# Attention over graph segments: the segment maxima are turned between columns and rows by VectorE, and the sets of zeros between gathers go

## The chip, the cores and the metric

The kernel runs on one core of a Trainium2 chip. A core has a matrix engine (TensorE, PE in the profile), a vector engine (VectorE, DVE), a scalar engine (ScalarE, ACT), a general engine that also issues the indirect gathers (GpSimd, POOL), and SyncE (SP), which issues plain transfers here. Each engine works through its own queue in order, and they wait for each other by semaphores. The metric is the device time of one execution in microseconds, the median of three runs.

## The reference

Four graph layers follow each other over 3125 nodes with 256 features and 100,000 edges sorted by destination. Layers 0 (two rounds) and 3 are graph attention with four heads. What is computed in one round of layer 0:

```python
e = jax.nn.leaky_relu(alpha_s[src] + alpha_d[dst], NEG_SLOPE)
m = jax.ops.segment_max(e, dst, num_segments=N)
ex = jnp.exp(e - m[dst])
s = jax.ops.segment_sum(ex, dst, num_segments=N)
alpha = ex / (s[dst] + 1e-16)
out = jax.ops.segment_sum(h[src] * alpha[:, :, None], dst, num_segments=N)
```

Layer 3 is the same with segments by source and each logit times the edge's weight. Layer 1 takes the logits from dot products of the two ends, and layer 2 sums messages without a softmax. Those two have code of their own.

## The kernel before

The work runs in stages behind each other. Three of them are calls of the function `attend`: tags `0a` and `0b` for the two rounds of layer 0 (kind "self", `own_max`: each node is also its own neighbour), and stage 3, whose names have no tag in the profile, for layer 3 (kind "weighted"). Edges are laid out in 816 units of 128, so that no unit crosses a group of 128 nodes. A turn handles STEP = 16 units in four quads of four, and there are 51 turns, three to a loop body.

A turn in `attend` goes like this. GpSimd gathers 128 table rows of 260 numbers for each unit into `ring` (L1520), which holds three turns. Behind each gather it sets a buffer named `pause` to zero (L1524, 128x256), which nobody reads; it waits by `paused` for its own sets of zeros and by `rows` for VectorE to free the ring. SyncE loads indices, masks and totals of units (`masks`, `totf`, `totb`, `tot_last`). TensorE turns the gathered scores so that 64 partitions (4 heads by 16 units) hold 128 edges each (`scores`), and VectorE adds the two parts (`y`, L1597), `leaky`, `withself` or `weigh`.

Then the maximum of each segment has to reach all its edges, also where a segment runs over several units. VectorE does this by scans. `fwd` scans each unit from its first edge; the last value of each unit goes to one line over the units, where `carried` scans it on and gives each unit the maximum it begins with (`begin`); `full` scans with that; `bwd` scans back; its first values go to a line again, `back` scans that, and gives `end`; `top` is then each edge's segment maximum. Between a column over 64 partitions and a line on one partition the numbers make a trip through TensorE: `trip1` to `trip4` (L1709), each a transpose into PSUM, and VectorE reads it back with a copy (`col1`, `begin`, `col2`, `end`, all at line L111 of a helper). `under`, `firsts` and `shrink` then make the differences, ScalarE takes `exp`, TensorE turns the result (`back_turned`) together with the factor by which the maximum has moved on, and ScalarE copies it out (`alphas`).

The same turn also sums the units of the turn before, while the maxima of this one are made. VectorE multiplies the gathered rows of a quad by their weights (`rows0` to `rows3`, L1577), ScalarE builds one-hot matrices of the edges' nodes in two steps (`away`, `hot`) and adds the weights' own columns (`ext`), TensorE multiplies the two (`mm0` to `mm15`, L1700, four PSUM banks in turn), and VectorE adds each result to its group of nodes (`add0` to `add15`, L1571). `factor` (L1672) and `rescale` (L1587) start the next turn's sums. The numbers of the groups come from a table and are loaded to registers in VectorE's queue (L1557) before `y`. TensorE also spreads the nodes' scores to edges (`spread0`, `spread1`), joins them (`joined`), and runs filler matmuls whose result nobody reads (`keep_busy`: 6 behind `scores`, 8 behind `trip2`, 8 behind `spread1`).

The order on each engine is written by hand: lists `V`, `A` and `M` name the steps of a turn on VectorE, ScalarE and TensorE. On VectorE the pieces of the maxima stand between the adds: `fwd`, `rows1`, `add0` to `add3`, `col1` to `carry`, `add4` to `add7`, `rows2`, `begin` to `bwd`, `rows3`, `add8` to `add11`, `col2`, `back`, `end` to `shrink`, `add12` to `add15`, `factor`. On ScalarE `exp` stands behind `hot3`, `ext3` (which wait for `mm7`) and `hot_r1`; `alphas`, `away0`, `hot0`, `parts`, `picked`, `own` follow.

## Time and profile before

| | us |
|---|---|
| median of three runs | 8620.68 |
| lowest and highest of them | 8600.65, 8642.47 |
| the profiled execution's own time | 8664.63 |
| its span, first to last instruction | 8662.7 |

| engine | busy, us | share of the span |
|---|---|---|
| TensorE, matmuls | 5621.8 | 65% |
| VectorE | 4989.0 | 58% |
| ScalarE | 3877.8 | 45% |
| GpSimd | 5844.0 | 67% |

Busy time is a sum over all stages, and no engine comes near the whole span, so what sets the time has to be read stage by stage, from the waits. A matmul's end is modelled in the profile; a time at which another engine goes on that waited for it is measured. Waiting and register instructions aren't counted as busy. Queues of plain transfers (SP) and of GpSimd's gathers share the 16 DMA engines; the gathers' queue took 27.5% of them and the other large one 9.3%.

### The profile page before, as it was taken

Reading aid. Unit: us, or ns where it says so; the run is one execution under the profiler, and the core shown is the slowest. Engines: PE = TensorE matmul, PEld = TensorE weight load, DVE = VectorE, ACT = ScalarE, POOL = GpSimd, SP = SyncE. Lnnn points to the kernel's source line nnn. Section 1 sums busy time; section 2 is a strip of 40 time slices with the busy share of each in tenths; the row PEclk is TensorE's granted clock in tenths of the full one; section 3 lists DMA queues with packets and bytes.
Section 4 is the critical chain, followed back from the end, with each engine's and each line's share of the span. In section 5 each row is a group of like instructions: output and inputs, shape, how many; then the busy total and the mean of one; then the engine's idle time right before and its main releaser. Section 6 shows DMA issues by size and latency. Waiting matters only on the chain. (4 is left out here: it accounts for less than half of the span.)

```text
span 8662.7 us, 136659 instructions
## 1 busy us (share of the span) xinstructions
PE 5621.8 (65%) x25128; PEld 3980.1 (46%) x25129; DVE 4989.0 (58%) x11551; ACT 3877.8 (45%) x9075; POOL 5844.0 (67%) x8186
## 2 busy tenths in 40 slices
PE   6442367667646666773677777748787763667765
PEld 5441244444424444442555555535555542444444
DVE  6445255556545555553777887754444444566666
ACT  2230255555424555552344444425555542555554
POOL 0556677777747777775466776757777765888884
PEclk9999687887767888776889998968888875788887
DMA  4111333333313333330466666523333322334442
GB/s 145 50 51 41 83 101 101 100 100 101 86 45 102 101 101 101 101 101 21 139 172 173 185 176 173 145 62 100 102 101 101 102 74 81 106 105 109 107 108 76
DMA packets 582372, 894.76 MB, mean 103 GB/s; under 512 B 308788, under 2 KB 359137, under 8 KB 581877
## 3 DMA queue, kind: packets, MB, share of 16 engines
q0 software_dynamic: 245984, 649.30, 27.5%
q1 hardware_dynamic: 335876, 218.84, 9.3%
q10 hardware_dynamic: 416, 25.60, 0.9%
q8 instruction: 30, 0.49, 0.0%
q14 instruction: 66, 0.53, 0.0%
HBM read 859.36 MB, written 59.47 MB: 106 GB/s over the span
## 5 line engine op out<-in xcount | busy, mean ns | idle before, releaser
L2024 POOL DMA_INDIRECT ad_ring<-tab_qv,ad_idx x808 | 768.8, 951 | 496.8 <-issue 242.1
L2440 POOL DMA_INDIRECT ae_ring<-tab_a,ae_idx x808 | 777.9, 963 | 399.4 <-PE ae_po L2597 199.9
L1520 POOL DMA_INDIRECT at_ring_0a<-tab_s,at_idx_0a x808 | 771.1, 954 | 368.6 <-DVE at_rows_0a L1577 207.3
L1520 POOL DMA_INDIRECT at_ring_0b<-tab_s,at_idx_0b x808 | 772.4, 956 | 349.8 <-DVE at_rows_0b L1577 174.1
L1520 POOL DMA_INDIRECT at_ring<-tab_s,at_idx x808 | 781.3, 967 | 272.8 <-issue 119.0
L2590 PE MATMUL ae_pM<-ae_we,ae_featT 64*128 64x256 f32 x1616 | 501.8, 461 | 211.2 <-issue 169.2
L1700 PE MATMUL at_po_0a<-at_rows_0a,at_hot_0a 128*128 128x264 f32 x1616 | 559.5, 504 | 101.1 <-DVE at_begin_0a L111 28.4
L1700 PE MATMUL at_po_0b<-at_rows_0b,at_hot_0b 128*128 128x264 f32 x1616 | 551.5, 499 | 110.7 <-DVE at_begin_0b L111 32.7
L1700 PE MATMUL at_po<-at_rows,at_hot 128*128 128x260 f32 x1616 | 540.9, 492 | 111.8 <-DVE at_begin L111 27.0
L2218 PE MATMUL ad_pk<-node_a,ad_hr 128*128 x1616 | 459.9, 433 | 210.7 <-DVE ad_prod L2101 107.7
L565 POOL DMA_INDIRECT recs_s<-rnk_recs_now,rnk_pos_now x294 | 288.3, 981 | 400.7 <-DVE rnk_both L465 178.2
L2590 PEld LDWEIGHTS ae_pM<-ae_we,ae_featT 64*128 64x128 f32 x1616 | 347.3, 226 | 348.3 <-issue 214.2
L2550 DVE TENSOR_TENSOR ae_pre<-ae_ring,ae_pM 128x1024 f32<-128x1024 f32 x202 | 246.7, 1221 | 445.4 <-PE ae_pM L2590 260.1
L2256 PE MATMUL ad_po<-ad_ring,ad_hot 128*128 128x264 f32 x1616 | 480.2, 429 | 32.4 <-ACT ad_hot L2329 11.5
L2597 PE MATMUL ae_po<-ae_msg,ae_hot 128*128 128x256 f32 x1616 | 453.2, 431 | 52.9 <-issue 37.6
L1700 PEld LDWEIGHTS at_po_0a<-at_rows_0a,at_hot_0a 128*128 128x128 f32 x1616 | 382.0, 249 | 218.3 <-issue 74.9
L1700 PEld LDWEIGHTS at_po_0b<-at_rows_0b,at_hot_0b 128*128 128x128 f32 x1616 | 375.9, 245 | 225.4 <-issue 72.4
L2397 DVE TENSOR_TENSOR acc<-acc,ae_po 128x256 f32 x808 | 290.8, 417 | 323.5 <-PE ae_po L2597 167.3
L1700 PEld LDWEIGHTS at_po<-at_rows,at_hot 128*128 128x128 f32 x1616 | 372.8, 243 | 216.3 <-issue 63.7
L2218 PEld LDWEIGHTS ad_pk<-node_a,ad_hr 128*128 128x128 f32 x1616 | 329.5, 213 | 306.2 <-issue 259.9
L1571 DVE TENSOR_TENSOR acc<-acc,at_po_0a 128x264 f32 x808 | 312.8, 421 | 231.7 <-PE at_pb_0a L1719 85.5
L1571 DVE TENSOR_TENSOR acc<-acc,at_po_0b 128x264 f32 x808 | 312.2, 421 | 209.8 <-PE at_pb_0b L1719 65.2
(538 smaller groups left out, 14649.4 us busy)
## 6 DMA issues: line engine op xcount, KB each, us to landing
at_rr_0a<-relrow_d SPq DMA_DIRECT2D x102, 256.0 KB
at_rr_0b<-relrow_d SPq DMA_DIRECT2D x102, 256.0 KB
ad_rr<-relrow_d SPq DMA_DIRECT2D x102, 256.0 KB
at_rr<-relrow_s SPq DMA_DIRECT2D x102, 256.0 KB
ae_feat<-attr_pad SPq DMA_DIRECT2D x808, 32.0 KB
rnk_lrow<-lorow_f SPq DMA_DIRECT2D x98, 256.0 KB
attr_pad<-in_edge_attr_dram ACTq DMA_DIRECT2D x1, 25000.0 KB, 79.3
at_ring_0a<-tab_s,at_idx_0a POOLq DMA_INDIRECT x808
```

What stands on the lines that cost most here:

```text
L565: eng.indirect_dma_start(out=order["s"]["recs"], out_offset=bass.IndirectOffsetOnAxis(ap=pos_now[:, t.slot, k:k + 1], axis=0), in_=recs_no ...
L1520: eng.indirect_dma_start(out=ring[:, t.slot * STEP + u, :], out_offset=None, in_=table, in_offset=bass.IndirectOffsetOnAxis(ap=idx[:, t.sl ...
L1571: v.did(f"add{u}", eng.tensor_tensor(to, to, po[:, u % 4:u % 4 + 1, 0:W], ALU.add))
L1700: m.did(f"mm{u}", eng.matmul(po[:, u % 4, 0:W], hot[:, q % 2, j, :], rows[:, q % 2, j, :, :].rearrange("p h f -> p (h f)"), start=True, st ...
L2024: eng.indirect_dma_start(out=ring[:, t.slot * STEP + u, :], out_offset=None, in_=table, in_offset=bass.IndirectOffsetOnAxis(ap=idx[:, t.sl ...
L2218: mm = eng.matmul(pk[:, p % 2, (u % 2) * D:(u % 2 + 1) * D], hot_r[:, u // HALF, (u % HALF) * P:(u % HALF + 1) * P], k_tab[:, bass.ds(gs[u ...
L2256: m.did(f"mm{u}", eng.matmul(po[:, u % 4, 0:W], hot[:, q % 2, j, :], ring[:, a.slot * STEP + u, D:D + W], start=True, stop=True))
L2397: own(eng.tensor_tensor(to, to, out_ps(q, j), ALU.add), False)
L2440: eng.indirect_dma_start(out=ring[:, k, :], out_offset=None, in_=table, in_offset=bass.IndirectOffsetOnAxis(ap=idx[:, k:k + 1], axis=0))\
L2550: own(eng.tensor_tensor(pre[:, q % 2, :, :].rearrange("p (a u) f -> p a (u f)", a=2), ring[:, q * QUAD:(q + 1) * QUAD, :].rearrange("p (a ...
L2590: mm = eng.matmul(pM[:, j // 2, (j % 2) * D:(j % 2 + 1) * D], featT[:, q % 2, j, :], We[:, :], start=True, stop=True)
L2597: mm = eng.matmul(po[:, (q % 2) * 2 + j // 2, (j % 2) * D:(j % 2 + 1) * D], hot[:, q % 2, j, :], msg[:, q % 2, j, :], start=True, stop=True)
```

## The change

In `attend` alone:

- The four trips through TensorE go. VectorE transposes blocks of 32 partitions by 32 columns itself (`turn1` to `turn4`). The lines over the units now lie on partitions 0 and 32, two heads each, with one place more for what is carried from turn to turn, so `line_f`, `run_f`, `totf` and their fellows have 64 partitions by 2 by 17 in place of 1 by 4 by 16. `fwd` is written backwards, so that its last value stands in column 0.
- VectorE's order changes: all of the maxima from `y` to `shrink` come in one piece, then `rows1`, `add0` to `add3`, `rows2`, `add4` to `add7`, `rows3`, `add8` to `add15`.
- TensorE's order changes: `back_turned` comes ahead of `mm12` to `mm15` and waits also for `rows3`. The eight filler matmuls behind `trip2` go.
- GpSimd no longer sets zeros between gathers, nor waits for them.
- `carry` is a copy of the run's last place; `tot_last` and its transfer go, and `totf` and `totb` are loaded for two partitions.

```diff
-            totf = sb(f"at_totf_{tag}", [1, BUFS, H, STEP], F32, c)
-            totb = sb(f"at_totb_{tag}", [1, BUFS, H, STEP], F32, c)
-            tot_last = sb(f"at_totl_{tag}", [1, BUFS], F32, c)
+            totf = sb(f"at_totf_{tag}", [R, BUFS, 2, STEP + 1], F32, c)
+            totb = sb(f"at_totb_{tag}", [R, BUFS, 2, STEP + 1], F32, c)
...
-            pause = sb(f"at_pause_{tag}", [P, 2, QUAD, 2 * P], F32, c)
...
-                        for w, to in ((0, totf[:, t.slot, :, 1:STEP]), (1, totb[:, t.slot, :, 0:STEP - 1])):
-                            eng.dma_start(to, od["totals"][w:w + 1, bass.ds(t.n * STEP + w, STEP - 1)]
-                                          .rearrange("w (o u) -> w o u", o=1).to_broadcast([1, H, STEP - 1]))\
+                        for w, to in ((0, totf[0:R:SQUARE, t.slot, :, 1:STEP + 1]), (1, totb[0:R:SQUARE, t.slot, :, 0:STEP])):
+                            eng.dma_start(to, od["totals"][w:w + 1, units_of(t)]
+                                          .rearrange("w (o u) -> w o u", o=1).to_broadcast([R // SQUARE, 2, STEP]))\
                                 .then_inc(masks_in[t.slot], 16)
-                        eng.dma_start(tot_last[:, t.slot:t.slot + 1], od["totals"][0:1, bass.ds(t.n * STEP + STEP - 1, 1)])\
-                            .then_inc(masks_in[t.slot], 16)
...
-                            eng.wait_ge(paused, t.n * STEP + (q * QUAD + QUAD))
...
-                                eng.memset(pause[:, q % 2, j, :], 0.0).then_inc(paused, 1)
-
-                    eng.sem_inc(paused, 2 * QUAD)
...
-                            v.did("fwd", eng.tensor_tensor_scan(fwd[:, :], brk, tops_in, -BIG, ALU.add, ALU.max))
-                        else:
-                            v.skip(*scored)
-                        weigh_rows(1)
-                        add(0, 1, 2, 3)
-                        if scores:
-                            eng.wait_ge(mat, m.at("trip1", t))
-                            v.did("col1", copy(eng, line_f[:, :, 1:STEP], row1_h[:, :, 0:STEP - 1]))
-                            done("col1", t)
+                            v.did("fwd", eng.tensor_tensor_scan(fwd[:, ::-1], brk, tops_in, -BIG, ALU.add, ALU.max))
+                            done("fwd", t)
+                            v.did("turn1", eng.transpose(line_f[:, :, 1:STEP + 1], fwd[:, 0:SQUARE].rearrange("r (h u) -> r h u", h=2)))
+                            done("turn1", t)
                             v.did("carried", eng.tensor_tensor_scan(line(run_f[:, :, :]), line(totf[:, t.slot, :, :]),
                                                                     line(line_f[:, :, :]), -BIG, ALU.add, ALU.max))
                             done("carried", t)
-                            v.did("carry", eng.scalar_tensor_tensor(
-                                out=line_f[:, :, 0], in0=run_f[:, :, STEP - 1], scalar=tot_last[:, t.slot:t.slot + 1],
-                                in1=row1_h[:, :, STEP - 1], op0=ALU.add, op1=ALU.max))
-                        else:
-                            v.skip("col1", "carried", "carry")
-                        add(4, 5, 6, 7)
-                        weigh_rows(2)
-                        if scores:
-                            eng.wait_ge(mat, m.at("trip2", t))
-                            v.did("begin", copy(eng, begin[:, :], col2))
-                            done("begin", t)
+                            v.did("turn2", eng.transpose(begin[:, :].rearrange("r (h u) -> r h u", h=2), run_f[:, :, 0:STEP]))
+                            done("turn2", t)
                             v.did("full", eng.tensor_tensor_scan(full[:, :], brk, tops_in, begin[:, 0:1], ALU.add, ALU.max))
                             done("full", t)
                             v.did("bwd", eng.tensor_tensor_scan(bwd[:, ::-1], brk_after, full[:, ::-1], -BIG,
                                                                 ALU.add, ALU.max))
-                        else:
-                            v.skip("begin", "full", "bwd")
-                        weigh_rows(3)
-                        add(8, 9, 10, 11)
-                        if scores:
-                            eng.wait_ge(mat, m.at("trip3", t))
-                            v.did("col2", copy(eng, line_b[:, :, 0:STEP - 1], row3_h[:, :, 1:STEP]))
-                            done("col2", t)
+                            done("bwd", t)
+                            v.did("turn3", eng.transpose(line_b[:, :, 0:STEP], bwd[:, 0:SQUARE].rearrange("r (h u) -> r h u", h=2)))
+                            done("turn3", t)
                             v.did("back", eng.tensor_tensor_scan(
                                 line(run_b[:, :, :])[:, ::-1], line(totb[:, t.slot, :, :])[:, ::-1],
                                 line(line_b[:, :, :])[:, ::-1], -BIG, ALU.add, ALU.max))
-                        else:
-                            v.skip("col2", "back")
-                        if scores:
-                            eng.wait_ge(mat, m.at("trip4", t))
-                            v.did("end", copy(eng, end[:, :], col4))
-                            done("end", t)
+                            done("back", t)
+                            v.did("turn4", eng.transpose(end[:, :].rearrange("r (h u) -> r h u", h=2), run_b[:, :, 1:STEP + 1]))
+                            v.did("carry", copy(eng, line_f[:, :, 0:1], run_f[:, :, STEP:STEP + 1]))
+                            done("turn4", t)
                             v.did("top", eng.tensor_tensor_scan(top[:, ::-1], brk_after, full[:, ::-1], end[:, 0:1],
                                                                 ALU.add, ALU.max))
                             done("top", t)
@@ -1662,10 +1632,16 @@
                                 done("under", t)
                                 v.did("firsts", eng.tensor_tensor(less[:, P:2 * P], less[:, P:2 * P],
                                                                   masks[:, t.slot, FIRST:FIRST + P], ALU.add))
-                            v.did("shrink", eng.tensor_scalar(less[:, EX:EX + 1], begin[:, :], top[:, 0:1], 0.0,
+                            v.did("shrink", eng.tensor_scalar(less[:, EX:EX + 1], begin[:, 0:1], top[:, 0:1], 0.0,
                                                               ALU.subtract, ALU.min))
                         else:
-                            v.skip(*under)
+                            v.skip(*scored, "turn1", "carried", "turn2", "full", "bwd", "turn3", "back", "turn4", "carry", *under)
+                        weigh_rows(1)
+                        add(0, 1, 2, 3)
+                        weigh_rows(2)
+                        add(4, 5, 6, 7)
+                        weigh_rows(3)
+                        add(8, 9, 10, 11)
...
-                        trip(1, "fwd", row1, fwd[:, P - 1:P], R)
                         reduce(1)
-                        trip(2, "carry", col2, line(run_f[:, :, :]), 1)
-                        if scores:
-                            keep_busy(eng, spare, 8)
                         reduce(2)
-                        trip(3, "bwd", row3, bwd[:, 0:1], R)
                         gs = None
                         if spreads:
                             _, gs = nc.values_load_multi_w_load_instructions(
                                 od["gof"][0:1, bass.ds((t.n + 1) * STEP, STEP)], engines=[ENG.PE], min_val=0, max_val=NB,
                                 skip_runtime_bounds_check_because="the table is clamped to NB on the chip")
                         spread(0, gs)
-                        trip(4, "back", col4, line(run_b[:, :, :]), 1)
-                        reduce(3)
                         if scores:
+                            if sums:
+                                eng.wait_ge(vec, v.at(f"rows{quads - 1}", t))
...
+                        reduce(3)
```

VectorE's queue, first stage, from `fwd` on, before:

```order
L1611 SCALAR_TENSOR_TENSOR at_fwd_0a<-at_masks_0a,at_tops_0a 64x128
L1577 TENSOR_TENSOR at_rows_0a<-at_ring_0a,at_pe_0a 128x16x64
L1568 REGISTER_ALU
L1537 REGISTER_ALU
L1571 TENSOR_TENSOR acc<-acc,at_po_0a 128x264
```

and now:

```order
L1602 SCALAR_TENSOR_TENSOR at_fwd_0a<-at_masks_0a,at_tops_0a 64x128
L1528 REGISTER_ALU
L1604 STREAM_TRANSPOSE at_linef_0a<-at_fwd_0a 64x2x16
L1528 REGISTER_ALU
L1606 SCALAR_TENSOR_TENSOR at_runf_0a<-at_totf_0a,at_linef_0a 64x34
L1528 REGISTER_ALU
L1609 STREAM_TRANSPOSE at_begin_0a<-at_runf_0a 64x32
```

The multiplication of rows and the adds stood right behind `fwd`; now the block transpose and the next scan do, and all the rest of the maxima.

VectorE's queue, from the copy or transpose of the backward maxima on, before:

```order
L111 TENSOR_SCALAR at_lineb_0a<-at_tt_0a 1x4x15
L1537 REGISTER_ALU
L1646 SCALAR_TENSOR_TENSOR at_runb_0a<-at_totb_0a,at_lineb_0a 1x64
L1652 REGISTER_ALU
L111 TENSOR_SCALAR at_end_0a<-at_tt_0a 64x1
L1537 REGISTER_ALU
L1655 SCALAR_TENSOR_TENSOR at_max_0a<-at_masks_0a,at_end_0a,at_full_0a 64x128
L1537 REGISTER_ALU
L1658 TENSOR_TENSOR at_less_0a<-at_log_0a,at_max_0a 64x256
L1537 REGISTER_ALU
L1663 TENSOR_TENSOR at_less_0a<-at_less_0a,at_masks_0a 64x128
L1665 TENSOR_SCALAR at_less_0a<-at_begin_0a,at_max_0a 64x1
```

and now:

```order
L1616 STREAM_TRANSPOSE at_lineb_0a<-at_bwd_0a 64x2x16
L1528 REGISTER_ALU
L1618 SCALAR_TENSOR_TENSOR at_runb_0a<-at_totb_0a,at_lineb_0a 64x34
L1528 REGISTER_ALU
L1622 STREAM_TRANSPOSE at_end_0a<-at_runb_0a 64x32
L112 TENSOR_SCALAR at_linef_0a<-at_runf_0a 64x2
L1528 REGISTER_ALU
L1625 SCALAR_TENSOR_TENSOR at_max_0a<-at_masks_0a,at_end_0a,at_full_0a 64x128
L1528 REGISTER_ALU
L1628 TENSOR_TENSOR at_less_0a<-at_log_0a,at_max_0a 64x256
L1528 REGISTER_ALU
L1633 TENSOR_TENSOR at_less_0a<-at_less_0a,at_masks_0a 64x128
```

The copies out of PSUM (`at_tt`), each of which waited for a trip, have become transposes (STREAM_TRANSPOSE) and one copy, and what comes after is no longer the last four adds but `rows1`.

TensorE's queue, around the transposes of the exponentials (`at_exp`), where `at_po` is a unit's matmul and `at_pb` a spread, before:

```order
L1699 REGISTER_ALU
L1700 MATMUL at_po_0a<-at_rows_0a,at_hot_0a 128x264
L1751 REGISTER_ALU
L1754 MATMUL at_pe_0a<-ident,at_exp_0a 128x64 x2
L1755 MATMUL at_pe_0a<-ident,at_exp_0a 128x4
L1714 REGISTER_ALU
L1719 ISA
L1719 MATMUL at_pb_0a<-b_tab,at_hr_0a 128x24
```

and now:

```order
L1688 MATMUL at_pb_0a<-b_tab,at_hr_0a 128x24
L1714 REGISTER_ALU
L1715 REGISTER_ALU
L1718 MATMUL at_pe_0a<-ident,at_exp_0a 128x64 x2
L1719 MATMUL at_pe_0a<-ident,at_exp_0a 128x4
L1674 REGISTER_ALU
L1675 REGISTER_ALU
L1676 MATMUL at_po_0a<-at_rows_0a,at_hot_0a 128x264
```

The transposes of the exponentials have moved from behind the last four units to ahead of them, right behind the first half of the spreads.

GpSimd's queue in the first stage, before:

```order
L1520 DMA at_ring_0a<-tab_s,at_idx_0a 128x260
L1524 MEMSET at_pause_0a 128x256
L1520 DMA at_ring_0a<-tab_s,at_idx_0a 128x260
L1524 MEMSET at_pause_0a 128x256
L1520 DMA at_ring_0a<-tab_s,at_idx_0a 128x260
L1524 MEMSET at_pause_0a 128x256
L1520 DMA at_ring_0a<-tab_s,at_idx_0a 128x260
L1524 MEMSET at_pause_0a 128x256
```

and now:

```order
L1513 DMA at_ring_0a<-tab_s,at_idx_0a 128x260 x4
L1509 REGISTER_ALU
L1513 DMA at_ring_0a<-tab_s,at_idx_0a 128x260 x4
L1509 REGISTER_ALU
L1513 DMA at_ring_0a<-tab_s,at_idx_0a 128x260 x4
L1509 REGISTER_ALU
```

The sets of zeros between gathers are gone, and the four gathers of a quad stand together.

## Rows read from the trace of the kernel before

**Rows 1.** View of one line (L1597, y): instructions, shortest/median/longest ns, first and last start
```profile
L1597 DVE TENSOR_TENSOR at_log_0a<-at_ta_0a,at_log_0a x51: 281/283/284, 1006.2 to 2411.9; 64x128 f32<-64x128 f32 x51
L1597 DVE TENSOR_TENSOR at_log_0b<-at_ta_0b,at_log_0b x51: 281/282/284, 2584.6 to 3974.4; 64x128 f32<-64x128 f32 x51
L1597 DVE TENSOR_TENSOR at_log<-at_ta,at_log x51: 281/282/285, 7308.1 to 8597.2; 64x128 f32<-64x128 f32 x51
```

**Rows 2.** View of stretches: busy us of each engine, granted clock, DMA share, GB/s
```profile
core 0: us, PE busy (x) PEld busy (x) DVE busy (x) ACT busy (x) POOL busy (x), PEclk, DMA share, GB/s
1034.00:2434.00 1400.00, 949.32 (x4229) 641.95 (x4229) 812.20 (x1958) 720.98 (x1700) 1014.09 (x1571) 0.79 0.36 94
```

**Rows 3.** View in order of time, POOL, first stage: start, us, instruction, idle before
```profile
1347.30 0.33 POOL L1524 MEMSET at_pause_0a<- 128x256 f32 x1
1347.78 0.95 POOL L1520 DMA_INDIRECT at_ring_0a<-tab_s,at_idx_0a  x1 [0.16 <-issue]
...
1354.79 0.95 POOL L1520 DMA_INDIRECT at_ring_0a<-tab_s,at_idx_0a  x1 [4.29 <-DVE at_rows_0a L1577]
```

**Rows 4.** Same view, POOL in the stage of dot products, which has no zeros
```profile
4623.38 0.95 POOL L2024 DMA_INDIRECT ad_ring<-tab_qv,ad_idx  x1 [0.31 <-issue]
```

**Rows 5.** Same view, DVE, one turn of the first stage
```profile
1328.88 0.28 DVE L1597 TENSOR_TENSOR at_log_0a<-at_ta_0a,at_log_0a 64x128 f32<-64x128 f32 x1 [2.06 <-PE at_po_0a L1700]
...
1330.27 1.19 DVE L1577 TENSOR_TENSOR at_rows_0a<-at_ring_0a,at_pe_0a 128x1024 f32<-128x1024 f32 x1
...
1333.58 1.45 DVE L1571 TENSOR_TENSOR acc<-acc,at_po_0a 128x264 f32 x4
...
1336.07 0.14 DVE L111 TENSOR_SCALAR at_begin_0a<-at_tt_0a 64x1 f32<-64x1 f32 x1
...
1337.10 1.19 DVE L1577 TENSOR_TENSOR at_rows_0a<-at_ring_0a,at_pe_0a 128x1024 f32<-128x1024 f32 x1
...
1345.27 0.15 DVE L111 TENSOR_SCALAR at_end_0a<-at_tt_0a 64x1 f32<-64x1 f32 x1 [2.64 <-PE at_po_0a L1700]
...
1346.83 0.43 DVE L1571 TENSOR_TENSOR acc<-acc,at_po_0a 128x264 f32 x1
1348.28 0.43 DVE L1571 TENSOR_TENSOR acc<-acc,at_po_0a 128x264 f32 x1 [1.02 <-PE at_pe_0a L1755]
1349.74 0.43 DVE L1571 TENSOR_TENSOR acc<-acc,at_po_0a 128x264 f32 x1 [1.03 <-issue]
1351.21 0.43 DVE L1571 TENSOR_TENSOR acc<-acc,at_po_0a 128x264 f32 x1 [1.05 <-DMA recs_s<-rnk_recs_now,rnk_pos_now]
...
1352.16 0.70 DVE L1587 TENSOR_TENSOR acc<-acc,at_pe_0a 128x528 f32 x1 [0.38 <-DVE at_pe_0a L1672]
...
1355.93 0.28 DVE L1597 TENSOR_TENSOR at_log_0a<-at_ta_0a,at_log_0a 64x128 f32<-64x128 f32 x1 [1.93 <-ACT at_log_0a L1854]
```

**Rows 6.** Same view, PE, the same turn
```profile
1333.94 1.48 PE L106 MATMUL at_ta_0a<-ident 128*128 128x384 bf16 x8
1336.38 2.04 PE L1700 MATMUL at_po_0a<-at_rows_0a,at_hot_0a 128*128 128x264 f32 x8 [0.96 <-ACT at_hot_0a L1789]
...
1343.10 3.57 PE L1700 MATMUL at_po_0a<-at_rows_0a,at_hot_0a 128*128 128x264 f32 x8 [0.15 <-issue]
1347.42 0.31 PE L1754 MATMUL at_pe_0a<-ident,at_exp_0a 64*128 64x64 f32 x2 [0.75 <-ACT at_exp_0a L1833]
```

**Rows 7.** Same view, ACT, the same turn
```profile
1334.50 1.26 ACT L1789 ACTIVATE at_hot_0a<-iota_row,at_nrel_0a 128x128 f32<-128x128 f32 x4
...
1336.57 1.13 ACT L1810 ACTIVATE at_hr_0a<-at_rr_0a,minus_col 128x1024 bf16<-128x1024 bf16 x1
...
1351.07 0.28 ACT L1835 ACTIVATE at_al_0a<-at_pe_0a 128x128 f32<-128x128 f32 x1 [3.80 <-DMA recs_s<-rnk_recs_now,rnk_pos_now]
```

**Rows 8.** View of line L1557: register loads in VectorE's queue
```profile
L1557 DVEq TENSOR_LOAD <-unit_of x306: 310/1100/3415, 1019.4 to 8612.4; - x153
```

**Rows 9.** Groups by line of the stretch 1034 to 2434: busy us, mean ns
```profile
L1620 DVE TENSOR_TENSOR_SCAN at_runf_0a<-at_totf_0a,at_linef_0a 1x64 f32<-1x64 f32 x50 | 13.9, 279 | 1.7
```

48 lines of the change are left out of this document (20 added, 28 removed).

## The prediction

> **What bounds the kernel now.** The change touches the three stages that run `attend` (tags 0a, 0b and 3), so I first took the length of their turns. The line of `y`, the first step of a turn's scores, starts 51 times in each stage [rows 1]: 0a from 1006.2 to 2411.9 is 50 turns of 28.1 us, 0b 50 of 27.8, stage 3 50 of 25.8. That is 4,085 us of the span of 8662.7. Then the stretches [rows 2]: in 0a no engine is busy through, VectorE 812 of 1400 us, GpSimd 1014, TensorE 949 as recorded, with TensorE's granted clock at 0.79 on average, so it moves between its two levels, 2.4 and 1.2 GHz. So a turn is a loop of waits, and I read one in order of time, from `y` at 1328.88 to the next at 1355.93, 27.05 us.
>
> GpSimd first [rows 3]. A gather takes 0.95, the zeros behind it 0.33, and 0.16 go by between: 1.44 a piece, 23.0 for the 16 of a turn. Then it stands for 4.29 us until VectorE's `rows` frees the ring. It isn't the bound; less work on it is worth nothing by itself.
>
> VectorE [rows 5]. After `y` come `rows1` (at +1.4), adds, the carried maxima in pieces, each after a trip through TensorE, and `rows3` at +8.2. The last trip comes back late: `end` starts at +16.4 after 2.64 us of waiting. From there `top` to `shrink` take 1.56, and the next add starts at 1346.83 (+17.95). The last four adds then start 1.45, 1.46 and 1.47 us apart, each after a pause of a microsecond. They wait for their matmuls. TensorE's records put those eight passes into 3.57 us from 1343.10 and the transposes of the exponentials at 1347.42 [rows 6], but ScalarE, which waits for just those, starts `alphas` at 1351.07 after 3.80 us [rows 7]. So the recorded ends are too early: TensorE was behind, and the loop runs through it. After the last add come `factor` and, at 1352.16, `rescale`; `y` follows 3.77 us later. In that gap VectorE's queue loads the 15 group numbers of the turn, a load of up to 3.4 us [rows 8].
>
> So the loop is: `y`, maxima, `exp`, TensorE's backlog, `alphas`, last adds, `rescale`, register load, `y`.
>
> **The change, part by part.**
>
> *The four trips become four block transposes.* Before, VectorE's part from `y` to the start of `rows1` is 1.39 us [rows 5], and the rest of the chain is spread behind adds. Now all of it stands in one piece ahead of `rows1`. Step by step: `y` to the end of `fwd` 1.39 + 0.11 (the next row may start before `fwd` ends, a dependent one may not) = 1.50; four transposes; the scans over the blocks' totals twice, 0.28 each [rows 9] and 0.04 to the next, 0.64; `full` and `bwd` 1.03 from 1336.07 to 1337.10 less 0.18 for `begin` plus 0.11, 0.96; `carry` 0.2; `top` to `shrink` 1.56 less 0.18 for `end`, 1.38. No row shows a block transpose. Its bounds are the 64x1 operation `end`, 0.15, and the 64x128 operation `y`, 0.28, twice that if it should run at half rate, 0.56. I take 0.20 plus 0.04, since it has 32 columns and so lies near the short one; four are 0.96. Sum: 1.50 + 0.96 + 0.64 + 0.96 + 0.20 + 1.38 = 5.64 us. The scans now run on 64 partitions by 34 columns in place of 1 by 64; fewer columns can only shorten them. A gain below nothing is not to be had from the transposes: they are work that VectorE didn't have.
>
> What this buys: `exp` no longer waits for a trip behind a backlog. What it costs: `rows1`, and with it units 4 to 7 on TensorE, start at +5.64 in place of +1.39, and ScalarE can't reach `exp` before it has done `hot3`, which waits for unit 7, and `hot_r1`. The code keeps that order on ScalarE.
>
> *The new loop,* with U for one unit (one tile's matmul, two records). `rows1` ends at 5.64 + 1.2 = 6.84. Units 4 to 7 follow: 4U. ScalarE: `away3`, `hot3`, `ext3` take 2.07 (1334.50 to 1336.57) and `far_r1`, `hot_r1` twice 1.13 and a bit, 2.30 [rows 7]. `exp` and its hand-overs 0.52; the transposes of `exp` 0.6 (0.31 for the first two passes [rows 6], twice). Units 12 to 15, now behind them: 4U. Last add, `factor` and `rescale`: 0.3 + 0.95 (1351.21 to 1352.16). Load and `y`: 3.77 [rows 5]. Sum: 6.84 + 2.07 + 2.30 + 0.52 + 0.60 + 1.25 + 3.77 = 17.35, plus 8U. `alphas` now comes before these units and waits for nothing; I take `parts` and `joined`, which come behind unit 15 as the load does, to end within the load's 3.77 us; if they don't, the turn grows by what they are over.
>
> *What U is.* The records give 2.04 / 4 = 0.51 for units 8 to 11 and 3.57 / 4 = 0.89 for units 12 to 15 [rows 6]; the last adds give 1.45 [rows 5]. An earlier four, queued behind other work, took 1.45 together, so their units were under that. No row settles the mean; I take the middle of 0.51 and 1.45, 0.98: the loop is then 17.35 + 7.84 = 25.2 us, 1.85 less than the turn read. In stage 3 the turn was 2.2 shorter already; with one table of exponentials less there I credit 1.4.
>
> *The zeros between gathers go.* GpSimd's own time isn't the bound. Without zeros a gather takes 0.95 with 0.31 ahead of it [rows 4], 1.26 or 20.2 us a turn. That becomes the floor of a turn; the forecast lies 5.0 above it, so GpSimd still waits for VectorE. But the distance of the adds, 1.45 to 1.47, is GpSimd's own cycle of 1.44 to the hundredths [rows 3, 5]. So the zeros may hold back TensorE's units. Bounds of what their going is worth: nothing, or all that lies between 1.45 and 0.51 per unit. The middle that I took for U has part of it in.
>
> By the Trainium skill ("SBUF — State Buffer", Who interferes with whom) TensorE never waits on any other engine, and GpSimd shares ports with VectorE alone. By that rule the zeros' going is worth nothing here and the match is chance. The adds' distance speaks against it, and no run yet shows which.
>
> *TensorE's load.* Gone are four small transposes and one of two sets of eight filler matmuls, 1.48 us as recorded [rows 6]. They stood ahead of unit 8; their going takes 1.5 us (2.6 at half clock) off the backlog. Units 8 to 11 aren't last in the new loop, so this is worth nothing beyond a safer order, but it makes TensorE stand idle from unit 3 to `rows1`, some 3 us in each turn.
>
> *The loads of masks* lose one small transfer a turn and spread two others over two partitions: off the path, 0.
>
> **Sum.** 50 x (1.85 + 1.85 + 1.4) = 255 us. The profiled execution took 8664.63, so 8410; the median lies 44 under it: **8365 us**.
>
> **The rivals.**
>
> *A: the zeros were the brake* and units fall to about 0.65. Turn 17.35 + 5.2 = 22.6; gain 4.5 x 150 = 667, 7955 us. For it: the match of cycles. Against it: GpSimd gathers all the same. Below 20.2 it can't go.
>
> *B: units stay slow.* If all eight units of the loop take the 1.45 of the last adds, a turn is 29.0: 150 x 1.95 = 290 us slower, 8910. The place is `rows1` behind the maxima, which lines up units 4 to 7 and 12 to 15 where before only the last four were waited for. It decides from U = (27.05 - 17.35) / 8 = 1.21. For it: the only distances seen in the adds. Against it: the four adds from 1333.58 took 1.45 us in all [rows 5].
>
> *C: the clock.* TensorE's granted clock is 0.79 now, and the change takes filler matmuls away and adds an idle stretch. Should it stay at 1.2 GHz: TensorE's 949 us in 1400 [rows 2] are 19.1 a turn of 28.1, or 15.1 at the full clock; less 1.5 for the fillers 13.6, at 1.2 GHz 27.2, and 3 idle: 30.2. That is 3.1 over the turn read, 470 us, 9090. The Trainium skill has this as a rule ("TensorE: Matmul & The Clock Gate", Part 1: throttled is the default, and activity releases the throttle).
>
> *D: no net effect,* U near 1.15 to 1.25: within 43 us of the median.
>
> **How the numbers follow.** The forecast has 0.55, A 0.18, D 0.11, B 0.09, C 0.07. Faster 0.73, the same 0.11, slower 0.16, with 0.5% (43 us) as what can be told from no change. The forecast's own range: U from 0.8 to 1.1 and transposes from 0.15 to 0.56 (on the path in full, so 4 x 0.36 = 1.4 a turn at worst) give 8150 to 8560. To hold eight in ten it goes to A's centre below and past D into the lower part of B above: 7950 to 8720.
>
> **What would show it.** `shrink` ends 5.6 us after `y` in the timeline; four transposes of 0.2; `exp` some 9 to 10 us after `shrink`, behind ScalarE's `hot_r1`. Turns of 25; gathers 1.26 apart and a longer wait of GpSimd. U from the distance of the last adds: at 1.45 B holds, at 0.65 A. The granted clock under 0.7 is C. Wrong would be the forecast if the next `y` were last behind `joined` rather than behind the load, or if `exp` came right after `shrink`.

## The result, and the profile after

The changed kernel took 9237.53 us, median of four runs (9223 to 9256), beside 8624.8 us for the kernel before in the same series: ratio 1.071, 95% interval 1.0687 to 1.0738. It is slower, and outside the range that was given. The profiled execution has a span of 9231.7 us, 569 more than before.

The line of `y` tells where. View of that line: instructions, shortest/median/longest ns, first and last start.

```profile
L1588 DVE TENSOR_TENSOR at_log_0a<-at_ta_0a,at_log_0a x51: 282/283/284, 1017.4 to 2552.8; 64x128 f32<-64x128 f32 x51
L1588 DVE TENSOR_TENSOR at_log_0b<-at_ta_0b,at_log_0b x51: 282/283/285, 2739.4 to 4277.3; 64x128 f32<-64x128 f32 x51
L1588 DVE TENSOR_TENSOR at_log<-at_ta,at_log x51: 282/283/284, 7606.6 to 9166.1; 64x128 f32<-64x128 f32 x51
```

A turn takes 30.7, 30.8 and 31.2 us in place of 28.1, 27.8 and 25.8 [rows 1]. Fifty times 2.6, 3.0 and 5.4 is 550 us, nearly the whole loss. The granted clock of TensorE went from 0.79 [rows 2] to 0.72 (view of stretches, same columns as there):

```profile
1034.00:2576.00 1542.00, 919.25 (x3634) 651.70 (x3634) 799.14 (x1956) 720.26 (x1701) 757.81 (x798) 0.72 0.32 86
```

One turn in order of time (start, us, instruction, idle before it). First VectorE, which answers to [rows 5]:

```profile
1503.85 0.28 DVE L1588 TENSOR_TENSOR at_log_0a<-at_ta_0a,at_log_0a 64x128 f32<-64x128 f32 x1 [2.03 <-issue]
...
1505.44 0.20 DVE L1604 STREAM_TRANSPOSE at_linef_0a<-at_fwd_0a 64x32 f32<-64x32 f32 x1
1505.68 0.22 DVE L1606 TENSOR_TENSOR_SCAN at_runf_0a<-at_totf_0a,at_linef_0a 64x34 f32<-64x34 f32 x1
...
1509.04 0.20 DVE L1635 TENSOR_SCALAR at_less_0a<-at_begin_0a,at_max_0a 64x1 f32<-64x1 f32 x1
1509.16 1.20 DVE L1568 TENSOR_TENSOR at_rows_0a<-at_ring_0a,at_pe_0a 128x1024 f32<-128x1024 f32 x1
...
1528.45 1.45 DVE L1562 TENSOR_TENSOR acc<-acc,at_po_0a 128x264 f32 x4 [10.66 <-DMA recs_s<-rnk_recs_now,rnk_pos_now]
...
1530.30 0.70 DVE L1578 TENSOR_TENSOR acc<-acc,at_pe_0a 128x528 f32 x1 [0.27 <-DVE at_pe_0a L1648]
...
1534.20 0.28 DVE L1588 TENSOR_TENSOR at_log_0a<-at_ta_0a,at_log_0a 64x128 f32<-64x128 f32 x1 [2.07 <-ACT at_hot_0a L1754]
```

Then ScalarE and TensorE, which answer to [rows 6, 7]:

```profile
1510.76 5.64 PE L1676 MATMUL at_po_0a<-at_rows_0a,at_hot_0a 128*128 128x264 f32 x16 [5.28 <-DVE acc L1562]
...
1518.97 0.40 ACT L1798 ACTIVATE at_exp_0a<-at_less_0a 64x257 f32<-64x257 f32 x1
...
1519.51 0.31 PE L1718 MATMUL at_pe_0a<-ident,at_exp_0a 64*128 64x64 f32 x2 [1.51 <-ACT at_hr_0a L1777]
...
1519.66 0.33 PE L1719 MATMUL at_pe_0a<-ident,at_exp_0a 64*128 64x4 f32 x2
...
1519.92 2.59 PE L1676 MATMUL at_po_0a<-at_rows_0a,at_hot_0a 128*128 128x264 f32 x8
...
1528.21 0.28 ACT L1800 ACTIVATE at_al_0a<-at_pe_0a 128x128 f32<-128x128 f32 x1 [8.84 <-DMA recs_s<-rnk_recs_now,rnk_pos_now]
```

The maxima run as forecast, `exp` follows 15.1 us behind `y`, and TensorE's records put the transposes of the exponentials half a microsecond later and units 12 to 15 right behind. Yet ScalarE gets to `alphas` only at 1528.21, after 8.84 us, and all four last adds come in one burst at 1528.45. The releaser named there, a transfer of another stage, can't be it; the profile put down the wait to what ended near it. What did end near it is GpSimd's row of gathers:

```profile
1511.16 0.94 POOL L1513 DMA_INDIRECT at_ring_0a<-tab_s,at_idx_0a  x1 [3.74 <-DVE acc L1562]
1512.40 0.95 POOL L1513 DMA_INDIRECT at_ring_0a<-tab_s,at_idx_0a  x1 [0.30 <-issue]
...
1524.91 0.95 POOL L1513 DMA_INDIRECT at_ring_0a<-tab_s,at_idx_0a  x1 [0.30 <-issue]
...
1532.93 0.94 POOL L1513 DMA_INDIRECT at_ring_0a<-tab_s,at_idx_0a  x1 [7.07 <-DVE at_rows_0a L1568]
```

Twelve gathers stand 1.25 us apart, the last ends at 1525.86, and `alphas` starts 2.35 later. Over 46 turns of this stage that distance was 2.33 us, between 2.28 and 2.36 in eight of ten. The waits of VectorE's adds and of `alphas` are the two longest in the loop (view of waits, 1034 to 2576: us in total, times, longest):

```profile
DVE acc L1562 <- DMA recs_s<-rnk_recs_now,rnk_pos_now: 525.6, 52, 17.6
ACT at_al_0a L1800 <- DMA recs_s<-rnk_recs_now,rnk_pos_now: 419.4, 47, 10.9
```

**Two conditions.** The kernel before took 8601 to 9000 us in four series and 7333 and 7345 us in two others, while the runs within a series agree. One chip gave 8641 in one series and 7345 in a later one, so this isn't a chip's own speed, though the expectations speak of machines. I call those four *late* and the two others *prompt*, and compare times within a series; where a comparison crosses two series, the text says so. The pair above is late. The difference isn't peculiar to `attend`: the stage of dot products, which no edit touches, takes 1375 to 1417 us from its first gather to its last in the fourteen late traces, and 1204 to 1207 in the six prompt ones.

### The profile page after: what moved, and what is told of

The parts are those of the page before. It is cut to its first block and busy times, and to the rows that moved or that the text cites. A ratio compares the mean times of both kernels' runs of the same rounds, so it can differ in the third digit from the quotient of the medians.

```text
span 9231.7 us, 128094 instructions
## 1 busy us (share of the span) xinstructions
PE 5572.6 (60%) x23292; PEld 4052.9 (44%) x23293; DVE 4954.7 (54%) x11551; ACT 3869.1 (42%) x9075; POOL 5035.6 (55%) x5762
## 3 DMA queue, kind: packets, MB, share of 16 engines
q0 software_dynamic: 245984, 649.30, 25.6%
## 5 line engine op out<-in xcount | busy, mean ns | idle before, releaser
L1676 PE MATMUL at_po<-at_rows,at_hot 128*128 128x260 f32 x1616 | 612.6, 551 | 303.0 <-DVE acc L1562 217.1
L1676 PE MATMUL at_po_0b<-at_rows_0b,at_hot_0b 128*128 128x264 f32 x1616 | 613.8, 551 | 257.6 <-DVE acc L1562 226.9
L1676 PE MATMUL at_po_0a<-at_rows_0a,at_hot_0a 128*128 128x264 f32 x1616 | 608.5, 547 | 263.7 <-DVE acc L1562 239.8
L1676 PEld LDWEIGHTS at_po<-at_rows,at_hot 128*128 128x128 f32 x1616 | 440.0, 283 | 434.8 <-DVE acc L1562 248.7
L1676 PEld LDWEIGHTS at_po_0b<-at_rows_0b,at_hot_0b 128*128 128x128 f32 x1616 | 435.1, 280 | 401.1 <-DVE acc L1562 260.4
L1676 PEld LDWEIGHTS at_po_0a<-at_rows_0a,at_hot_0a 128*128 128x128 f32 x1616 | 430.5, 277 | 404.5 <-DVE acc L1562 265.4
L1562 DVE TENSOR_TENSOR acc<-acc,at_po 128x260 f32 x808 | 300.8, 417 | 568.2 <-DMA recs_s<-rnk_recs_now,rnk_pos_now 501.3
```

The source lines that it names most:

```text
L1562: v.did(f"add{u}", eng.tensor_tensor(to, to, po[:, u % 4:u % 4 + 1, 0:W], ALU.add))
L1676: m.did(f"mm{u}", eng.matmul(po[:, u % 4, 0:W], hot[:, q % 2, j, :], rows[:, q % 2, j, :, :].rearrange("p h f -> p (h f)"), start=True, st ...
```

## The experiments

My theory after the result, H: a row of gathers without zeros keeps TensorE's results from the other engines. Its rivals: O, the new order costs; K, the half clock behind the idle stretch costs.

### First series: zeros back, zeros taken from before

e1 puts the zeros behind each gather again, e3 makes them 128x1, e4 sets one 128x256 per quad:

```diff
+                                eng.memset(pause[:, q % 2, j, :], 0.0).then_inc(paused, 1)
```

e2 takes this line and its waits out of the kernel before, and changes nothing else.

> The changed kernel with the sets of zeros (128x256) back behind each gather, and nothing else. Theory H (a row of gathers without anything between them keeps TensorE's completions from being seen until the row ends): alphas no longer starts 2.3 us after the last gather, the 8.8 us wait before it falls to 2 to 4 us, a turn is 24 to 26 us, the kernel takes 8250 to 8500 us. Theory O (the new order of steps is slow by itself, because units 4 to 7 and 12 to 15 line up behind the maxima): a turn stays at 30 to 31 us, 9150 to 9300 us.

> The kernel before without the sets of zeros in attend, trips and order as they were. Theory H: the four trips and alphas each wait for the end of a row of gathers, so it is slower than before by at least 5%, 9050 us or more, and perhaps slower than the changed kernel. Theory O: GpSimd was not the bound, so within 1% of 8625 us.

> The changed kernel with a set of zeros of one column (128x1) behind each gather. If what matters is that some other GpSimd instruction stands between two gathers, it does what e1 does (8250 to 8500 us, perhaps less, since gathers are then closer). If what matters is the time that GpSimd gives (0.33 us a gather), the hold stays in most part: 8900 us or more. Theory O: 9150 to 9300 us.

> The changed kernel with one set of zeros (128x256) behind each fourth gather. Theory H with a hold that lasts as long as an unbroken row: TensorE's completions come once a quad, every 5.4 us, so alphas waits about 4 us, a turn is 26 to 28 us, 8450 to 8850 us. If only the share of time matters, 9100 us. Theory O: 9150 to 9300 us.

Measured, with before at 7333.18 (prompt): e1 7481, ratio 1.020 (1.0183 to 1.0217); e2 6901, 0.941 (0.9393 to 0.9425); e3 7460, 1.018 (1.0161 to 1.0195); e4 7474, 1.019 (1.0175 to 1.0209). No hold of any kind. The waits in e3 (ScalarE, in order of time) are those that the chain asks for:

```profile
1430.70 0.40 ACT L1803 ACTIVATE at_exp_0a<-at_less_0a 64x257 f32<-64x257 f32 x1
1431.76 0.28 ACT L1805 ACTIVATE at_al_0a<-at_pe_0a 128x128 f32<-128x128 f32 x1 [0.66 <-PE at_pe_0a L1724]
```

So H as a law of the chip falls: here before gains 6% without its zeros. And the new order in e3, at the same cycle of 1.25 us, takes 559 us more than e2. That spoke for O, though e3 differs from e2 also by its block transposes and the eight fillers that it lacks. The 7% of the first pair stayed unexplained.

### Second series: the change again, and its parts in the old order

e5 is the change, e6 the kernel before. e7 has the block transposes and no zeros, but VectorE's and TensorE's order and the eight fillers of before; e8 is the change with those fillers:

```diff
-             + ["rows1", "add0", "add1", "add2", "add3", "rows2", "add4", "add5", "add6", "add7", "rows3",
+        V = (["rescale", "rows0"] + scored + ["rows1", "add0", "add1", "add2", "add3", "turn1", "carried", "turn2",
+             "add4", "add5", "add6", "add7", "rows2", "full", "bwd", "rows3",
...
+                            keep_busy(eng, spare, 8)
```

> The changed kernel as it is, beside the kernel before on the same chip. Theory H (an unbroken row of gathers keeps TensorE's results back, wherever the program runs): slower than before by about the 7% of the first pair, alphas starts 2.2 us after the last gather of a row, after some 8.8 us of waiting. Theory M (the delay of results belongs to the machine of the first pair, where units of before came 0.72 and 1.44 us apart; in the four runs so far they came 0.43 and 0.87 us apart): no such wait, a turn as with the tiny sets of zeros (23.8 us), since GpSimd's cycle was 1.25 us there as well, so about 7460 us, 2% slower than before.

> The kernel before as it is, for its trace on this chip. Theory M: the last adds of a turn stand 0.43 or 0.87 us apart and the turn is about 22 us, as the time of 7333 us asks. Theory H: adds 1.45 us apart as in the first trace, with the gain over it somewhere outside attend. If the time is near 8620, the machine of the first pair has been met again.

> VectorE's block transposes in place of the trips and no sets of zeros, but VectorE's and TensorE's order and the eight fillers as before the change. If the new order is what costs (theory O), this is as fast as before without zeros: the gathers run back to back there (20.3 us a turn), so 6900 us and no less, ratio 0.94 to before. If the block transposes themselves cost (theory X), it stays near 7400.

> The changed kernel with the eight filler matmuls back ahead of units 8 to 11 (behind fwd). Theory K: the 6 us in which TensorE stands still during the maxima, and the half clock after them, are what costs. The fillers stand behind units 0 to 7 and don't fill them, so this alone gains nothing: 7460 to 7560. If the clock recovers by them, 7200.

Before took 8640.63 here (late). e5: 9238.68, ratio 1.068 (1.0659 to 1.0709), so the first result holds, and so does the hold: `alphas` starts 2.31 us after the last gather's end (median of the stage) after 8.8 us of waiting. e7: 9178, 1.061 (1.0576 to 1.0642): in this condition the old order doesn't save it, and the loss comes with what e5 and e7 share. e8: 9268, 1.072 (1.0705 to 1.0743): the fillers mend nothing. That is no test of K as a whole, since they stand behind units 0 to 7 and leave TensorE's idle stretch as it was. e6: 8642, turns of 27.7, 27.4 and 25.9.

e5's trace shows something else. Register steps of TensorE's own queue that took 46 ns in the first series take up to 1.4 us here; in the first stage of e5, 208 of some 960 took 0.6 to 0.8 us, in that of e1 none. The same line of the first traced change and of e1 (shortest/median/longest ns):

```profile
L1688 PEldq FUSED_REGOPS  x2448: 3/46/1383, 983.3 to 9158.4; - x189
```

```profile
L1693 PEldq FUSED_REGOPS  x2448: 46/46/51, 825.1 to 7408.5; - x189
```

Gathers take 0.95 us in both, so what is late isn't the gathers. But these long steps are not the cause of the hold, nor the mark of the condition. In the first stage they (FUSED_REGOPS in the profile) appear only in the new order with gathers 1.25 us apart, and not alike there (193 in the first traced change, 208 in e5, 220 in e11, but 8 in e8); in e7 and e10, whose results are held too, and in all other late traces there are none. What does tell the conditions apart is SyncE's queue. Its register moves reach 0.69 to 1.40 us in the first stage of every late trace and 0.04 us in that of every prompt one. The same line of the kernel before (e6, late) and of e18 (prompt):

```profile
L1461 SPq MOVE at_masks_0a<-masks_d x192: 3/29/715, 1013.1 to 2305.2; - x192
```

```profile
L1461 SPq MOVE at_masks_0a<-masks_d x192: 29/29/29, 859.8 to 2005.6; - x192
```

### Third series: zeros and order apart, in the late condition

e9 is e1's kernel, e10 is e2's, e11 is e3's. e12 is e7 with its full zeros.

> The changed kernel with one set of zeros of 128x256 behind each gather again, as in before (the kernel of e1_zeros_back), meant for the machine of the first pair (before near 8630 us). In its traces steps of TensorE's and SyncE's queues took 0.69 us each time and again (208 of TensorE's 956 register steps in the first attend of e5, none of 923 where before takes 7333 us). Theory H: an unbroken row of gathers there lets TensorE's messages through hardly at all, and the zeros' pause lets one or two through per gather. Then the last set's hold goes: turns of 30.8 fall to 25 to 27 us, 8350 to 8700 us in all. Theory O (the new order alone costs): 9240, as without zeros. On the machine of 7333 us: 7480 again.

> The kernel before with only the zeros and their waits left out, meant for the machine of the first pair. Theory H: turns of 30 us as in the run with turns in the old order (e7), 9150 to 9250 us, slower than before by 6 to 7%. Theory O: 8620 or faster. On the machine of 7333 us: 6900 again.

> The changed kernel with a set of zeros of 128x1 behind each gather: GpSimd's cycle stays 1.25 us as without zeros. On the machine of the first pair: if the length of the pause between gathers is what lets TensorE's messages through, this is as slow as the change, 9200 to 9250; if it is that GpSimd does anything else between two gathers, it is as fast as with the full zeros, 8350 to 8700. On the other machine: 7460 again.

> Block transposes in place of the trips, everything else as before: VectorE's and TensorE's order, fillers and full zeros. It prices the transposes alone. On the machine of the first pair, theory H: no trips to wait for, so at most the 8600 of before, 8200 to 8500 us; if the messages of TensorE are what paces the turn, four fewer of them a turn help too. If it is above 8700, block transposes cost something of their own. On the machine of 7333 us: GpSimd's cycle of 1.44 us makes 23 us a turn at least for 16 gathers, so nothing to gain, 7250 to 7340.

Before: 8600.82 (late). e9: 8864, ratio 1.030 (1.0268 to 1.0336). e10: 9387, 1.090 (1.0865 to 1.0929). e11: 9248, 1.075 (1.0723 to 1.0777). e12: 8622, 1.002 (1.0004 to 1.0042).

This is what parts the change. Taking the zeros away costs 9% in before as it is (e10) and 4% in the new order (e9 to e11, 385 us, here with tiny zeros), and, across two series, 6% in the old order with transposes (e12 to e7). Tiny zeros are as bad as none, so it isn't that GpSimd does something between two gathers, it is how long it pauses: the cycle is 1.25 us with tiny zeros and 1.44 with full ones. The new order, with the eight fillers gone, costs 2.8% on top (e9 beside e12), where I had expected e9 at 8350 to 8700. So within this one series the steps from before are +22 us for the transposes (e12), +241 for the new order (e9) and +385 for the shorter pause (e11). The transposes by themselves are worth nothing here, and e12 shows why (TensorE, ScalarE and VectorE in order of time):

```profile
1517.45 0.42 ACT L1815 ACTIVATE at_exp_0a<-at_less_0a 64x257 f32<-64x257 f32 x1 [4.61 <-DVE at_less_0a L1649]
...
1518.01 0.31 PE L1736 MATMUL at_pe_0a<-ident,at_exp_0a 64*128 64x64 f32 x2 [1.85 <-ACT at_exp_0a L1815]
...
1520.10 0.43 DVE L1568 TENSOR_TENSOR acc<-acc,at_po_0a 128x264 f32 x1 [1.75 <-PE at_pb_0a L1703]
...
1522.45 0.43 DVE L1568 TENSOR_TENSOR acc<-acc,at_po_0a 128x264 f32 x1 [1.92 <-DMA recs_s<-rnk_recs_now,rnk_pos_now]
...
1523.96 0.28 ACT L1817 ACTIVATE at_al_0a<-at_pe_0a 128x128 f32<-128x128 f32 x1 [6.09 <-DMA recs_s<-rnk_recs_now,rnk_pos_now]
```

`exp` comes 2.7 us sooner behind `y` than before (15.4 in place of 18.1, medians of 40 turns), but `alphas` stays at 22.2 beside 22.3: the late results take it all back. (Before's medians are those of the first traced run, from another late series.)

The medians of 40 turns of the first stage, from the start of `y` to the start of each step, in us (e15 belongs to the next series):

| kernel | condition | `shrink` | `exp` | `alphas` | last four adds | `rescale` | next `y` |
|---|---|---|---|---|---|---|---|
| before | late | 17.8 | 18.1 | 22.3 | 18.0 to 20.9 | 23.5 | 27.4 |
| the change | late | 5.2 | 15.1 | 24.3 | 24.6 to 25.6 | 26.4 | 30.3 |
| e9, change with zeros | late | 5.2 | 15.0 | 16.7 | 17.7 to 22.3 | 23.2 | 27.6 |
| e12, transposes alone | late | 15.2 | 15.4 | 22.2 | 17.3 to 21.0 | 23.3 | 27.2 |
| e15, transposes alone, longer zeros | late | 14.9 | 15.1 | 18.1 | 15.8 to 17.4 | 19.4 | 25.3 |
| e3, change, tiny zeros | prompt | 5.2 | 15.1 | 16.2 | 17.0 to 18.6 | 19.7 | 23.6 |
| e2, before, no zeros | prompt | 13.0 | 13.2 | 15.8 | 13.1 to 15.2 | 16.9 | 20.7 |

### Fourth series: moving the gathers, a longer pause, more signals

e13 is the change, and e14 is e7, with GpSimd's row held back until `factor`:

```diff
-                            eng.wait_ge(vec, v.at(f"rows{q}", t.plus(-2)))
+                            eng.wait_ge(vec, v.at("factor", t.plus(-2)))
```

e15 is e12 with longer zeros, and in e16, the kernel before, the eight fillers behind `spread1` add to a semaphore each:

```diff
+            pause = sb(f"at_pause_{tag}", [P, 2, QUAD, 352], F32, c)
...
+                mm.then_inc(said, 1)
```

> The changed kernel, no zeros, but GpSimd waits with each turn's 16 gathers until VectorE has done factor two turns back, in place of rows0 to rows3 of that turn. The 16 gathers take 20.2 us from there, so none runs between exp (15 us behind y, about 20 us behind factor) and the next factor. Theory H: with the gathers gone from it the wait of alphas falls from 8.8 to about 1 us and the last adds come 0.43 or 0.87 us apart; a turn of 24 to 25.5 us in place of 30.8, 8250 to 8450 us on the machine of the first pair, faster than before (8600 to 8640). If the hold belongs to the place in TensorE's queue and not to the gathers: 30 us or more, above 9200. On the machine of 7333 us 20.2 us and exp to factor in a row make 24.5: 7500 to 7600.

> The same, with VectorE's and TensorE's order and fillers of before, block transposes, no zeros (e7 with its gathers behind factor). Theory H: in place of 29.8 us a turn 24 to 25 us, 8200 to 8400 us on the machine of the first pair. In the old order more of TensorE's results fall in the first 16 us behind y, beside the row, so if those are held instead, 27 us and more: 8600 or above.

> e12 (block transposes, old order, zeros) with zeros of 128x352 in place of 128x256, so GpSimd's cycle is about 1.56 us in place of 1.44 and a turn at least 25 us. If the length of the pause is what lets messages through (1.25 us cycle: 9178 us, 1.44: 8622), a longer one brings more: 8350 to 8550 us on the machine of the first pair. If one gap per gather of any length above some amount is enough, 8600 to 8700, since the gaps come more seldom. On the machine of 7333 us the floor of 25 us a turn: 7550 to 7650.

> The kernel before, in which each of the eight filler matmuls behind spread1 also adds one to a semaphore that nobody waits for: eight more messages from TensorE a turn and no more work. If it is the messages that pass at a fixed pace beside the gathers (one in 0.7 to 1.4 us), joined and with it y come later, by up to 5.8 to 11 us a turn less what parts and the register load cover (3 to 4 us): 8900 to 9800 us on the machine of the first pair. If the matmuls themselves are late, or on the machine of 7333 us, nothing: within 0.5% of before.

Before: 9000.03 (late, and more so than the others). e13: 9455, ratio 1.050 (1.0463 to 1.0531). e14: 9687, 1.076 (1.0722 to 1.079). e15: 8406, 0.933 (0.9297 to 0.9359). e16: 8990, 0.999 (0.9973 to 1.0012).

e13 missed the times that I expected, e14 met only the second of its two (8600 or above, if the results beside the row are held instead), and that is what its trace shows: the hold went with the row. In e14, whose gathers ran from 1545.48 to 1565.20 without a gap, VectorE's adds of units 0 to 3 stood 2.9 to 4.3 us apart, and with the row's end units 4 to 7 came in a burst:

```profile
1557.11 0.43 DVE L1563 TENSOR_TENSOR acc<-acc,at_po_0a 128x264 f32 x1 [5.02 <-DMA recs_s<-rnk_recs_now,rnk_pos_now]
1559.98 0.43 DVE L1563 TENSOR_TENSOR acc<-acc,at_po_0a 128x264 f32 x1 [2.44 <-PE at_po_0a L1686]
1564.25 0.43 DVE L1563 TENSOR_TENSOR acc<-acc,at_po_0a 128x264 f32 x1 [3.84 <-DMA recs_s<-rnk_recs_now,rnk_pos_now]
1567.76 0.43 DVE L1563 TENSOR_TENSOR acc<-acc,at_po_0a 128x264 f32 x1 [3.08 <-DMA recs_s<-rnk_recs_now,rnk_pos_now]
...
1568.89 1.45 DVE L1563 TENSOR_TENSOR acc<-acc,at_po_0a 128x264 f32 x4
```

```profile
1545.48 0.95 POOL L1514 DMA_INDIRECT at_ring_0a<-tab_s,at_idx_0a  x1 [9.77 <-DVE at_pe_0a L1658]
...
1564.25 0.94 POOL L1514 DMA_INDIRECT at_ring_0a<-tab_s,at_idx_0a  x1 [0.30 <-issue]
```

With no gathers left, `alphas` followed `exp` by 1.1 us there (median of 40 turns). What I gained behind `exp` I lost at the units ahead of it, and more: `exp` came 28.1 us behind `y`.

e15 has 0.57 us from the end of a gather to the next in place of 0.49. With it the hold is gone in some turns and shorter in the rest: `alphas` comes 2.9 us behind `exp` (median of 40 turns, 14 of them under 1.5) where e12 had 6.2, none under 1.5. A turn without it, in which the last adds come in one row of 1.43 us and `alphas` 1.07 behind `exp`:

```profile
1600.70 0.42 POOL L1521 MEMSET at_pause_0a<- 128x352 f32 x1
1601.28 0.95 POOL L1517 DMA_INDIRECT at_ring_0a<-tab_s,at_idx_0a  x1 [0.16 <-issue]
1602.22 0.42 POOL L1521 MEMSET at_pause_0a<- 128x352 f32 x1
1602.80 0.95 POOL L1517 DMA_INDIRECT at_ring_0a<-tab_s,at_idx_0a  x1 [0.17 <-issue]
```

```profile
1600.77 1.43 DVE L1568 TENSOR_TENSOR acc<-acc,at_po_0a 128x264 f32 x4
...
1600.88 0.42 ACT L1815 ACTIVATE at_exp_0a<-at_less_0a 64x257 f32<-64x257 f32 x1 [0.59 <-DVE at_less_0a L1649]
1601.95 0.28 ACT L1817 ACTIVATE at_al_0a<-at_pe_0a 128x128 f32<-128x128 f32 x1 [0.66 <-PE at_pe_0a L1737]
```

Its turns are 25.8, 25.7 and 24.4 us, over the 24.3 of sixteen gathers 1.52 apart. How much the longer pause is worth by itself isn't shown, since e12 wasn't run in this series: beside its own before e15 gains 6.7%, but this before was the slowest of all, and 8406 is 2.3% under the 8601 of the third series. e16 refutes what I had made of the 0.7 us steps: eight more signals a turn cost nothing, so it isn't that each signal holds the queue for 0.7 us or more.

### Fifth series: the same pause under the whole change and under before

e17 is the change with zeros of 128x352, e18 the kernel before with 128x336.

> The changed kernel with zeros of 128x352 behind each gather. Where before takes 8600 to 9000 us: if the pause ends the hold in the new order too, alphas follows exp within 1.5 us, the last adds are 0.4 to 0.9 us apart and the gathers' 16 times 1.52 us bound the turn at 24.5 to 25.5 us: 8300 to 8400 us, even with or a little better than e15. If the new order's half clock behind the maxima costs on its own, 8450 to 8600. Where before takes 7333 us: 7500 to 7600, bound by the gathers.

> The kernel before with zeros of 128x336 in place of 128x256 (a cycle of about 1.51 us), nothing else. If the gain of e15 is the pause's alone, 8400 to 8500 us where before takes 8600 to 9000; if it needs the four trips gone too (they add four results of TensorE to a turn, each waited for), 8600 to 8800. Where before takes 7333 us: 7450 to 7550, bound by the gathers.

Before: 7344.99 (prompt). e17: 7558, ratio 1.029 (1.0273 to 1.0307); e18: 7505, 1.022 (1.0201 to 1.0236). Both are bound by GpSimd: turns of 24.4 and 24.2 us at cycles of 1.52 and 1.51. Neither was run in the late condition, so whether e15's gain needs the transposes beside the pause, and what that pause does in the new order, stays open.

In sum, as ratios to before of the same series:

| maxima and order | condition | no or tiny zeros | 128x256 | 128x336 or 352 |
|---|---|---|---|---|
| trips, old order | late | 1.090 | 1 | |
| transposes, old order | late | 1.061 | 1.002 | 0.933 |
| transposes, new order | late | 1.068 to 1.075 | 1.030 | |
| trips, old order | prompt | 0.941 | 1 | 1.022 |
| transposes, new order | prompt | 1.018 | 1.020 | 1.029 |

No version that was run in both conditions beats before in both. e15, which was run in the late one alone, is the fastest there, and e2 in the prompt one.

## Why the prediction was wrong

**What held.** `shrink` ended 5.39 us behind `y` (5.64 forecast); a block transpose of 64x32 took 0.20 us and the 64x34 scan 0.22; `exp` came 9.7 us behind its end, in the 9 to 10 given; gathers stand 1.25 us apart; the register load and `y` took 3.90 behind `rescale` (3.77). The sum stood as far as `exp`: 6.84 + 3.92 + 2.07 + 2.30 is 15.13, and `exp` started 15.1 us behind `y`. All that was missed lies behind it: 10.06 forecast, 15.2 measured in the change, 12.5 in e9, 8.5 in e3.

**The step that failed** is "Bounds of what their going is worth: nothing, or all that lies between 1.45 and 0.51 per unit". It had no side below nothing. The adds' distance that equalled GpSimd's cycle [rows 3, 5] was a sign that the row of gathers paces TensorE's results, though the turn that I read wasn't typical: of the last four adds' 120 distances in 40 turns, 18 lay at 1.38 to 1.52 us and 61 under 0.5. I read it as the zeros braking. In the late condition it was the gathers, and the zeros were the pause that let the results through. Taking them away cost 385 us in the new order (e11's 9248 beside e9's 8864, one series; e5's 9239 agrees) and 786 in the old one (e10 beside before). By the same step "`alphas` now comes before these units and waits for nothing" was wrong by 8.84 us in the turn shown, 8.8 in the median. Behind it stands a reading: "the recorded ends are too early: TensorE was behind". The trace's record of semaphore updates speaks against a slow TensorE. In the first stage of every late trace 27 to 218 pairs of neighbouring updates by TensorE's steps stand 0.06 us apart or less, and in the prompt traces no two are nearer than 0.108. Such bunches are signals that waited, not units that took long, so no value of U could describe them.

The rule that I weighed from the Trainium skill ("SBUF — State Buffer", Who interferes with whom: TensorE never waits on any other engine) gives nothing for the zeros' going. The new order in the prompt condition agrees with it (e1 and e3, 1.020 and 1.018). The late one doesn't (e10, 1.090; e11 beside e9), and there the measurement decides; whether what is held there waits for a port of the memory, which is what that section is about, no run shows.

**The second step that failed** is U and what it was set against. I took the old turn as read, 27.05 us, and put a middle U of 0.98 under the new loop alone. By the new loop's own sum, 17.35 + 8U, U was 0.78 in e3 (23.6 us, prompt), 1.28 in e9 (27.6) and 1.62 in the change (30.3). These are the forecast's own unit cost fitted afterwards, and they hold a wait that isn't a unit's. But the old order, unheld, takes 20.7 us (e2), 2.9 less than the new one with the same cycle of gathers (e3), although e3 has the transposes; and in the late condition, with the same zeros, e9 takes 241 us more than e12. So in the late condition the new order is the longer one by itself, and in the prompt one it is so with the transposes and fillers changed along with it. I priced `rows1` going from +1.4 to +5.6 in the new loop but never asked what the old loop would be at that U. Units 4 to 7 reach their adds at 8.9 to 11.0 behind `y` in place of 4.8 to 5.8, and units 12 to 15 stand behind `exp` in place of beside the maxima. How the 2.8% of the order splits between this and the lower granted clock (0.73 in e9's first stage, 0.78 in e12's) isn't shown.

**The rivals.** B, units that stay slow, comes near e9: it decided from U = 1.21, e9's was 1.28, and its 8910 lies 46 over e9's 8864. That is half luck. Of its eight units the last four came slowly (1.2 to 2.0 us apart in e9's medians), while units 4 to 7 came as early as in the prompt e3. The change itself went past B, by a hold that no rival had. A was read off the same sign with the wrong direction. C's turn of 30.2 us and its 9090 lie nearest to what was measured (30.3 and 9238), and that is luck: the clock averaged 0.72, where C asks for 1.2 GHz throughout, and e9, at 0.73 and with the same order, took 385 us less than e11 at 0.71. TensorE's idle stretch behind the maxima was 5.28 us in the turn shown, where the forecast had some 3. In e3 units 6 and 7, behind that stretch, come 0.9 us apart and the last four 0.4 to 0.7; that speaks for some half clock in the order's price, which no run took away.

## What to carry to other kernels

When a wait's spacing equals another engine's cycle, the two may be coupled, but the sign of what follows from removing part of that cycle isn't given: price it on both sides, and try it alone. Read the spacing over all turns, not in one. Work that seems idle may be a pause that others live on. Run the kernel before in every series: the same program took 7333 and 9000 us here, and an edit that gained 6% in one series cost 9% in another. And when an order is changed, put the same unit cost under the old loop and under the new before taking the difference.
